# A graph layer on Trainium2: attention weights of 14 supertiles turned by a transposing transfer instead of by TensorE

## What is computed

```python
h = jnp.maximum(_layernorm(x, axis=-1), 0.0)
hi_t = h @ W1_w[:HID] + dep_emb @ W1_w[HID:] + W1_b      # per pair i, j
hj_t = h @ W2_w[:HID] + dep_emb @ W2_w[HID:] + W2_b
masked = jnp.where(adj, jnp.sum(hi_t * hj_t, axis=-1), NEG)
A = jax.nn.softmax(masked, axis=2)
aggregated = jnp.einsum('bij,bjd->bid', A, h)
h_syn = jax.nn.relu(aggregated @ gcn_w + gcn_b)
out = x + h_syn @ Wo_w + Wo_b
```

## Time and profile before

| | |
|---|---|
| median of 3 runs | 362.43 us (362.26 to 362.5) |
| profiled execution, its own time | 362.2 us |
| its span in the trace | 360.4 us |
| PE busy | 350.2 us, 97% of the span |
| ACT busy | 272.1 us, 76% |
| DVE busy | 262.4 us, 73% |
| POOL busy | 175.4 us, 49% |
| granted TensorE clock | 1.0 of full speed |

### The profile page before, as it was taken

The page is one execution under the profiler, slowest core; times in us unless marked ns, Lnnn a source line. Parts: engine busy times, 40 slices in busy tenths (PEclk is TensorE's granted clock), DMA queues, the critical chain, the costliest instruction groups (busy, mean ns, idle before and its releaser), DMA issues.

```text
span 360.4 us, 9432 instructions
## 1 busy us (share of the span) xinstructions
PE 350.2 (97%) x3124; PEld 217.1 (60%) x3124; DVE 262.4 (73%) x664; ACT 272.1 (76%) x577; POOL 175.4 (49%) x353
## 2 busy tenths in 40 slices
PE   7999989999999999999999999999999999999986
PEld 7766465565657566565656566565756666565753
DVE  0998798586958677685958777695968767586664
ACT  3398896978787887778797877778698877855742
POOL 2067473746547182746637183755628183770000
PEclk9999999999999999999999999999999999999999
DMA  7994607965557493855557393645548363544053
GB/s 226 322 201 144 178 12 164 201 150 175 126 137 178 99 250 88 227 111 163 128 136 195 87 262 87 203 113 151 146 130 218 87 175 89 104 110 139 2 145 119
DMA packets 82216, 53.88 MB, mean 149 GB/s; under 512 B 45666, under 2 KB 82148, under 8 KB 82196
## 3 DMA queue, kind: packets, MB, share of 16 engines
q1 hardware_dynamic: 81488, 53.22, 57.2%
q10 hardware_dynamic: 644, 0.20, 0.3%
q0 software_dynamic: 64, 0.20, 0.2%
HBM read 17.44 MB, written 12.58 MB: 83 GB/s over the span
## 4 chain that ended last, share of the span: by engine, by line
PE 88%; ACT 4%; DVE 4%; DMA 2%; issue 1%; DVEq 0%; SPq 0%; ACTq 0%
PE bank L1156 24%; PE bank L1157 24%; PE bank L1158 24%; PE bank L1407 3%; PE bank L1402 3%; PE bank L1259 3%; PE bank L1267 2%; DMA x_all<-in_L_gnn_W_w_dram 2%; PE bank L1200 2%; PE bank L1373 1%; ACT bank L637 1%; ACT h_tok L481 1%; PE bank L1469 1%; PE bank L1471 1%; ACT h_parts L481 1%
## 5 line engine op out<-in xcount | busy, mean ns | idle before, releaser
L433 POOL TENSOR_TENSOR h_parts<-h_tok,h_parts 128x1536 f16<-128x1536 f32 (+1 forms) x15 | 43.6, 2905 | 94.6 <-ACT h_parts L481 94.5
L1156 PE MATMUL bank<-gw_hi,hT 128*128 128x385 f16 x192 | 63.0, 328 | 1.4 <-DVE g_parts L911 0.9
L409 POOL TENSOR_TENSOR x_all<-x_all,bo_all 128x1536 f32 (+1 forms) x16 | 55.0, 3441 | 15.9 <-ACT h_tok L499 15.9
L1158 PE MATMUL bank<-gw_hi,hT 128*128 128x385 f16 x192 | 62.7, 327 | 0.0
L1157 PE MATMUL bank<-gw_lo,hT 128*128 128x385 f16 x192 | 62.5, 326 | 0.0
L1156 PE MATMUL bank<-wo_hi,z_hi 128*128 128x384 f16 x180 | 58.8, 327 | 0.5 <-DVE z_lo L1032 0.5
L1158 PE MATMUL bank<-wo_hi,z_lo 128*128 128x384 f16 x180 | 58.7, 326 | 0.0
L1157 PE MATMUL bank<-wo_lo,z_hi 128*128 128x384 f16 x180 | 58.7, 326 | 0.0
L1156 PE MATMUL bank<-hT,m_hi 128*128 128x512 f16 x144 | 54.6, 379 | 0.7 <-DVE hT L734 0.7
L1157 PE MATMUL bank<-hT,m_hi 128*128 128x512 f16 x144 | 54.6, 379 | 0.0
L1158 PE MATMUL bank<-hT,m_lo 128*128 128x512 f16 x144 | 54.6, 379 | 0.0
(11 more groups left out here) (163 smaller groups left out, 678.3 us busy)
## 6 DMA issues: line engine op xcount, KB each, us to landing
x_all<-in_x_dram SPq DMA_DIRECT2D x16, 768.0 KB, 6.2
out_dram<-x_all SPq DMA_DIRECT2D x15, 768.0 KB, 4.5
hg_parts<-hg_lo SPq DMA_DIRECT2D x32, 192.0 KB, 3.4
hg_parts<-hg_hi SPq DMA_DIRECT2D x32, 192.0 KB, 3.9
x_all<-in_L_gnn_W_w_dram SPq DMA_DIRECT2D x2, 576.0 KB, 5.1
out_dram<-x_all SPq DMA_DIRECT2D x4, 192.0 KB, 1.9
gcn_raw<-in_L_gnn_gcn_w_dram SPq DMA_DIRECT2D x1, 576.0 KB, 10.6
x_all<-in_L_gnn_Wo_w_dram SPq DMA_DIRECT2D x1, 576.0 KB, 11.3
```

Source lines behind the costliest of these rows:

```text
L409: nc.gpsimd.tensor_tensor(x_all[:, s, :, :], x_all[:, s, :, :], bo_all[:, :, :].broadcast_to([P, KT, D]), ALU.add).then_inc(x_biased, 1)
L433: ins = nc.gpsimd.tensor_tensor(h_parts[:, at, 1, :], h_tok[:, at, :], h_parts[:, at, 0, :], ALU.subtract)
L1156: nc.tensor.matmul(dst, lh, rh, start=(c == 0), stop=False)
L1158: last = nc.tensor.matmul(dst, ll, rh, start=False, stop=(c == DC - 1))
```

## The change

For the attention weights of supertiles 1 to 14 the turning is no longer done by PE. DVE writes, between the high and the low part, a second copy of the high part into a buffer `att_spread`, in which the weights of graph 0 stand in the first 64 columns of a tile and those of graph 1 in the last 64, with zeros elsewhere (zeroed once at the start by POOL). `att_parts` and `att_spread` lie side by side in `att_all`, 128 partitions by 1024 f16 columns. SP then issues one transposing transfer from `att_all` to `attT_all` (8 blocks of 128 x 128), which holds both `attT_parts` and `attT_hi`. PE's four transposes, ACT's copy and DVE's two copies of these rounds go. `aggregation` waits for the transfer (`attT_landed`) instead. Supertiles 0 and 15 are treated as before.

```diff
+        att_all = sb("att_all", [P, KT, 2, 2, S], f16)
+        att_parts = att_all[:, :, 0, :, :]
+        att_spread = att_all[:, :, 1, :, :]
+        attT_all = sb("attT_all", [P, KT, 2, GT, S], f16)
+        attT_parts = attT_all[:, :, 0, :, :]
+        attT_hi = attT_all[:, :, 1, :, :]
...
+            def transpose_attention(s):
+
+                sp.wait_ge(att_ready, s + 1)
+                sp.wait_ge(att_spread_made, GT * s)
+                sp.wait_ge(att_cleared, 1)
+                sp.wait_ge(z_done, DC * s)
+                sp.dma_start_transpose(attT_all[:, :, :, :, :].rearrange("p k b g i -> p (k b) (g i)"),
+                                       att_all[:, :, :, :, :].rearrange("p k b g i -> p (k b g i)"))\
+                  .then_inc(attT_landed, 16)
...
                 move_hg(s + 1)
+                if s + 1 < LAST:
+                    transpose_attention(s + 1)
                 store_out(s)
...
             def iteration(s, nxt2=True):
                 for c in range(DC):
                     g_high_part(s, c)
-                    if c == 1:
-                        attention_out(s)
                     g_whole(c)
...
+                if isinstance(s, int) and s == 1:
+                    dve.wait_ge(attT_done, 1)
+                    dve.wait_ge(att_cleared, 1)
+                elif not isinstance(s, int) or s > 1:
+                    dve.wait_ge(attT_landed, 16 * (s - 1))
                 nc.vector.tensor_scalar(att_parts[:, :, 0, :], scores[:, :, :], A_SCALE, None,
                                         ALU.mult).then_inc(att_high, 1)
+                if not isinstance(s, int) or 1 <= s < LAST:
+                    for g in range(GT):
+                        rows = slice(g * S, (g + 1) * S)
+                        nc.vector.tensor_scalar(att_spread[rows, :, g, :], scores[rows, :, :], A_SCALE, None,
+                                                ALU.mult).then_inc(att_spread_made, 1)
...
             def iteration(s, nxt2=True):
                 g_low_part(s, 0)
-                attention_high(s)
                 g_low_part(s, 1)
...
             def aggregation(s, z_bank):
 
-                pe.wait_ge(attT_high, GT * s)
-                pe.wait_ge(attT_copied, s)
+                if isinstance(s, int) and s in (1, LAST + 1):
+                    made = 1 if s == 1 else 2
+                    pe.wait_ge(attT_high, GT * made)
+                    pe.wait_ge(attT_copied, made)
+                else:
+                    pe.wait_ge(attT_landed, 16 * (s - 1))
...
                     g_chunk(c, half, chunk_ready(s) if c == 0 else None)
-                    if c == 1:
-                        transposed_attention(s)
```

More of the change, by code:

```diff
@@ L151, in gnn_layer_program @@
         row_inv = sb("row_inv", [P, KT])
-        att_parts = sb("att_parts", [P, KT, 2, S], f16)
-        attT_parts = sb("attT_parts", [P, KT, GT, S], f16)
-        attT_hi = sb("attT_hi", [P, KT, GT, S], f16)
+        att_all = sb("att_all", [P, KT, 2, 2, S], f16)
[4 more added lines that the diff above has]
+        attT_hi = attT_all[:, :, 1, :, :]
         z_hi = sb("z_hi", [P, DC, N], f16)
@@ L211, in gnn_layer_program @@
         names = """score_copied summed masked hg_moved attT_copied attT_cleared ident16_made weighted
-            att_high w1_loaded w2_loaded dep_loaded gcn_loaded wo_loaded bo_loaded adj_loaded
+            att_high att_spread_made att_cleared attT_landed w1_loaded w2_loaded dep_loaded gcn_loaded wo_loaded bo_loaded adj_loaded
             adj_rest_loaded gcn_b_loaded x_loaded ident_zeroed e_one e_loaded ident_made ones_made
@@ L224, in gnn_layer_program @@
         (score_copied, summed, masked, hg_moved, attT_copied, attT_cleared, ident16_made, weighted,
-         att_high, w1_loaded, w2_loaded, dep_loaded, gcn_loaded, wo_loaded, bo_loaded, adj_loaded,
+         att_high, att_spread_made, att_cleared, attT_landed, w1_loaded, w2_loaded, dep_loaded, gcn_loaded, wo_loaded, bo_loaded, adj_loaded,
          adj_rest_loaded, gcn_b_loaded, x_loaded, ident_zeroed, e_one, e_loaded, ident_made,
@@ L332, in _ @@
             nc.gpsimd.memset(attT_hi[:, :, :, :], 0.0).then_inc(attT_cleared, 1)
+            nc.gpsimd.memset(att_spread[:, :, :, :], 0.0).then_inc(att_cleared, 1)
             def coefficients(s, stats, mul, add, counted):
@@ L613, in _, with attention_out @@
                 act.wait_ge(ty_free, NSUP + 1)
[L615 to L619, removed]
+            def attention_out(n):
+                act.wait_ge(attT_done, n)
+                if n == 2:
+                    act.wait_ge(z_done, DC * LAST)
                 nc.scalar.activation(attT_parts[:, :, :, :], attT_bank[:, :, :, :],
@@ L698, in _ @@
             iteration(LAST, nxt2=False)
-            attention_out(LAST + 1)
+            attention_out(2)
             for c in range(DC):
@@ L1016, in _, with attention_high @@
                     nc.vector.sem_inc(ty_free, 1)
[L1018 to L1023, removed]
+            def attention_high(n):
+                dve.wait_ge(attT_copied, n)
+                if n == 1:
+                    dve.wait_ge(attT_cleared, 1)
                 else:
-                    dve.wait_ge(attT_cleared, 1)
+                    dve.wait_ge(z_done, DC * LAST)
                 for g in range(GT):
@@ L1067, in masked_scores, with attention @@
                                         ALU.mult).then_inc(exp_bias_ready, 1)
-            def attention(s, prev=True):
+            def attention(s):
                 dve.wait_ge(exp_done, KT * (s + 1))
@@ L1076, in attention @@
                 dve.wait_ge(weighted, s + 1)
-                if prev:
-                    dve.wait_ge(attT_done, s)
+                if isinstance(s, int) and s == 1:
[3 more added lines that the diff above has]
+                    dve.wait_ge(attT_landed, 16 * (s - 1))
                 nc.vector.tensor_scalar(att_parts[:, :, 0, :], scores[:, :, :], A_SCALE, None,
                                         ALU.mult).then_inc(att_high, 1)
+                if not isinstance(s, int) or 1 <= s < LAST:
[3 more added lines that the diff above has]
+                                                ALU.mult).then_inc(att_spread_made, 1)
                 dve.wait_ge(att_high, s + 1)
@@ L1094, in second_round @@
                 wo_low_part(0)
-                attention(0, prev=False)
+                attention(0)
                 g_low_part(1, 2)
                 wo_low_part(1)
-                attention_high(1, prev2=False)
+                attention_high(1)
                 part_statistics(3, range(KT))
@@ L1137, in _ @@
             iteration(LAST, nxt2=False)
-            attention_high(LAST + 1)
+            attention_high(2)
             for c in range(DC):
@@ L1365, in transposed_attention @@
                 pe.wait_ge(att_ready, s)
-                if not isinstance(s, int) or s >= 2:
-                    pe.wait_ge(attT_high, GT * (s - 1))
-                    pe.wait_ge(attT_copied, s - 1)
-                else:
-                    pe.wait_ge(ident16_made, 1)
+                if s == 1:
+                    pe.wait_ge(ident16_made, 1)
+                else:
+                    pe.wait_ge(attT_high, GT)
+                    pe.wait_ge(attT_copied, 1)
                 for k in range(KT):
```

## The result

| | before | after |
|---|---|---|
| median of the runs | 362.47 us (362.26 to 362.53, 6 runs) | 359.89 us (359.82 to 360.1, 6 runs) |
| span of the profiled execution | 360.4 us | 358.1 us |
| a round of the middle, early and late | 20.48, 20.47 us | 20.25, 20.25 us |

The ratio is 0.9928, with a 95% interval of 0.9914 to 0.9943. The change makes the kernel 2.58 us faster. The forecast was 2.9 us, and 359.5 us as the time. The two profiled executions, 362.2 and 359.88 us, differ by 2.3 us only, as their spans do: the one of the kernel before was faster than the median of its runs. In later timings one run of the kernel before and two of the kernel with 8 blocks ahead took 455 to 607 us at a granted clock of 0.76 or less, and no median here holds them.

What follows compares the result with a forecast made beforehand. PE was taken as the bound, busy throughout the middle rounds; 13 x 0.22 = 2.86 us off the median of 362.43 us, other edits 0, gave 359.5 us, 0.8% faster, with a range of 358.9 to 361.2 us.

Steps and rivals of the forecast that it cites:

- The bound: Middle rounds: PE is busy throughout at the full granted clock; a round was to take 20.26 us.
- 0.22 us for four transposes, thirteen times: PE between second and third chunk: four transposes leave, 0.22 us a round in thirteen rounds, 2.86 us.
- The sum outside the rounds: Start and tail: edits there, such as POOL's extra clearing, are not on the path and cost 0.
- DVE's pair at 0.85 us: DVE between high and low part: two new instructions take 0.85 us, leaving 0.43 us ahead of PE's third chunk.
- that rival: DVE's insertion reaches PE: at 1.70 us for the pair, third chunk stalls 0.42 us, 365.0 us; 5%.
- The transfer at 3.1 us: SP's new transfer ahead of the aggregation: lands 3.1 us after issue, 1.22 us issue plus 1.85 us fixed, 1.8 us early.
- The 4.9 us of budget: Ahead of the aggregation: the new transfer may take up to 4.9 us at no cost; from 5.1 us slower.
- The rival of the late transfer: PE waits for the transfer ahead of the aggregation: 367 or 385 us; 8%, plus 2% for a block-by-block transfer.
- The transfer of h: On SP behind the new transfer: issue unmoved, landing 1 to 1.5 us later, covered before hT's readers; cost 0.
- Round 2: PE's wait for DVE's g subtraction grows from 0.88 to 1.1 us, so this round gains nothing.

Runs made afterwards that it cites:

- the kernel with 8 blocks ahead: Changed kernel plus a transposing transfer of 8 blocks of zeros, read by nobody, issued just ahead of the attention weights' transfer: 360.47 us, ratio 0.9949.
- the kernel before with ACT's edit: Kernel before, with ACT doing the last two tiles of supertile 3's normalisation behind round 2's first g chunk: 362.33 us, ratio 1.0.
- The attempt to win it on ACT: Changed kernel, with ACT doing the last two tiles of supertile 3's normalisation behind round 2's first g chunk: 360.66 us, ratio 0.9964.

## Why the prediction was right, and what it missed

- **The bound.** Right: PE busy throughout at the full granted clock, a round of 20.25 us for 20.26 forecast.
- **0.22 us for four transposes, thirteen times.** Right to 0.04 us in all: 2.90 us for 2.86. The kernel that puts the four products back, and nothing else, shows it from the other side: 20.48 us again. Reading starts and not durations decided this term: the row's 0.39 us would have given 5.1 us.
- **The sum outside the rounds.** This is the step that was short. The forecast took start and tail to be untouched; they give back 0.2 and 0.38 us. The 0.38 us go with DVE's program: in six of the fourteen profiles of this study the additions start 0.76 us after the last products, in the other eight, all with the changed kernel's DVE program, 1.14 or 1.15 us after them, and six instructions at the head, with their buffer, turn the one into the other. That it is the position of the instructions and not that of a buffer is likely and not shown, and neither is how it makes the delay. The 0.2 us stay open. Both profiles of the kernel before have the weights landing at 7.50 us. The other twelve have them at 7.67 to 8.35, with the clearing ahead of them and without it, the kernel before with ACT's edit (7.67) among them.
- **DVE's pair at 0.85 us.** Right: 0.86 us. The additions end at 206.42, the third chunk starts at 206.89, which leaves 0.47 us (0.43 forecast). Doubling the pair turned it into a loss of 0.46 us a round and made the kernel 0.7% slower, 365.19 us for the 365.0 of that rival. Part of this agreement is luck: the rival had thirteen rounds of 0.2 us, and it was twelve of 0.25 us less 0.22 us in the last.
- **The transfer at 3.1 us.** Right, from a third of a longer transfer's issue (1.25 us for 1.22) plus its fixed part (1.85 us). It landed 1.8 us ahead of its reader, as forecast. The Trainium skill (VectorE: DVE Perf Modes, The three transpose paths and Rules for kernel authors) has 1309 ns for a 128 x 128 turn through DMA, an estimated 10.5 us for eight one after another. Here the eight are all there 3.1 us after the issue, 0.39 us each, and no wait follows, so its rule that TensorE is the choice did not hold in this kernel, where PE is the bound and the transfer has 4.9 us.
- **The 4.9 us of budget.** Borne out: PE loses 0.89 us when the aggregation can start only 5.8 us after the low part. The forecast took a landing as readable at once; PE starts some 0.25 us after it. The rival of the late transfer was a true danger and not a far one. SP's order alone, the store first, brings it about, and costs 19 us against the changed kernel.
- **The transfer of h.** The size was off and a reader was missed. It lands 1.8 us later at the median and not 1 to 1.5, and behind it stands ACT's normalisation, 2.5 us after the landing in the round shown, and not only PE's first g product of the next round. It cost nothing here, but eight more blocks of traffic made it wait.
- **Round 2.** Right: the wait grew from 0.88 to 1.08 us and the round gained nothing. The attempt to win it on ACT shows that chains through POOL and DVE are as tight there.

## What to carry to other kernels

Where PE is busy throughout, four small products are worth what the starts around them show, and copies taken from ACT and DVE are worth nothing. A turn by DMA can hide such work, if its issue stands ahead of other transfers on the same queue and the slack is counted from the write that it waits for; look on all engines for what waits for each transfer that it delays, those that overwrite a source too. When a sum is right and the span still differs by a few tenths of a us, compare start and tail row by row before a new cause is sought in the rounds.

## What was not expected of the hardware

- The delay from the start of the last products to the additions on DVE is 0.76 or 1.14 us, with the same instructions and waits, and six one-column memsets at the head of DVE's program, with the buffer they write, choose between them.
- Counted by starts, a wait costs PE some 0.15 us more than the idle time in its row: 0.46 us for 0.31, 0.89 for 0.73.
- A transposing transfer of 8 blocks takes 1.25 us of SP's issue and lands after 3.1 us with idle DMA engines. Right behind a store it takes 2.04 us and lands after 4.5 us. Right behind another of 16 blocks its issue takes 1.89 us, and it lands after 3.7 us at the median; behind one of 8 blocks, 1.34 and 3.2 us.
